# Layer norm scaling moved from VectorE to GpSimd, behind its own power, in a four-layer gated attention kernel

## The reference

```
def _layernorm(x, axis=-1, eps=1e-05):
    m = jnp.mean(x, axis=axis, keepdims=True)
    v = jnp.var(x, axis=axis, keepdims=True)
    return (x - m) / jnp.sqrt(v + eps)
...
    x = x + jnp.tanh(g_xattn[0]) * _L0_xattn_ref(_layernorm(x, axis=-1), ...)
    x = x + jnp.tanh(g_ffn[0]) * _L0_ffn_ref(_layernorm(x, axis=-1), ...)
```

## Time and profile before

| | |
|---|---|
| time, three runs | 2367.44 us median (2361.81 to 11244.14) |
| the profiled execution | 2362.89 us, span 2360.8 us, mean TensorE clock 0.952 |
| busy | PE 2068.2, PEld 1614.0, DVE 1973.1, ACT 1476.0, POOL 959.0 us |
| HEADS block, one pass | 136.5 us |
| WIDE block, one pass | 136.5 us |

### The profile page before, as it was taken

The page is one execution under the profiler, slowest core; times in us unless marked ns, Lnnn a source line. Parts: engine busy times, 40 slices in busy tenths (PEclk is TensorE's granted clock), DMA queues, the critical chain, the costliest instruction groups (busy, mean ns, idle before and its releaser), DMA issues. The chain is left out here.

```text
span 2360.8 us, 41642 instructions
## 1 busy us (share of the span) xinstructions
PE 2068.2 (88%) x12569; PEld 1614.0 (68%) x12569; DVE 1973.1 (84%) x7820; ACT 1476.0 (63%) x3639; POOL 959.0 (41%) x1382
## 2 busy tenths in 40 slices
PE   5878788989989899989999899998999899797767
PEld 3556567657966688656876578765886578666545
DVE  1299897989989798998989898897989899896971
ACT  3546467666767666776666666676667767476431
POOL 3233214543354424554164434544255432433432
PEclk9979899999999999999999999999999999899877
DMA  4000101010100101001100101001100001001000
GB/s 184 1 8 1 34 24 32 1 34 1 55 4 1 34 19 39 1 1 35 55 3 1 34 6 52 1 1 34 32 26 1 6 23 55 30 4 52 1 3 3
DMA packets 29503, 55.03 MB, mean 23 GB/s; under 512 B 2914, under 2 KB 10082, under 8 KB 28642
## 3 DMA queue, kind: packets, MB, share of 16 engines
q1 hardware_dynamic: 29282, 52.37, 6.8%
HBM read 51.31 MB, written 1.05 MB: 22 GB/s over the span
## 5 line engine op out<-in xcount | busy, mean ns | idle before, releaser
L232 DVE MATCH_REPLACE8 top_work<-top_eight,top_work 128x256 f32<-128x256 f32 x1664 | 668.4, 409 | 0.0
L234 DVE MAX8 top_eight<-top_work 128x8 f32<-128x256 f32 x1664 | 618.0, 413 | 0.2
L268 POOL TENSOR_TENSOR top_p<-top_p,top_rest 128x512 f32<-128x512 f32 x192 | 244.4, 1273 | 161.4 <-ACT top_rest L261 161.4
L789 PE MATMUL bank<-workP 128*128 128x256 f32 x1024 | 275.5, 393 | 12.4 <-ACT att_pP L927 10.2
L927 ACT ACTIVATE att_pP<-bank,att_tinyP 128x256 f32<-128x256 f32 x512 | 216.0, 480 | 57.1 <-DVE att_tinyP L976 55.3
L789 PEld LDWEIGHTS bank<-workP 128*128 128x128 f32 x1024 | 179.4, 192 | 62.2 <-issue 30.7
L976 DVE TENSOR_REDUCE att_tinyP<-bank 128x2 f32<-128x512 f32 x256 | 173.7, 682 | 25.5 <-PE bank L789 23.5
L234 DVE MAX8 top_lead<-bank 128x8 f32<-128x256 f32 x384 | 145.1, 420 | 42.1 <-PE bank L594 17.8
L261 ACT ACTIVATE top_rest<-top_work,top_nmax 128x256 f32<-128x256 f32 x384 | 173.3, 503 | 11.2 <-DVE top_work L232 10.9
L240 POOL TENSOR_SCALAR top_nmax<-top_lead 128x2 f32<-128x2 f32 x192 | 37.1, 193 | 346.4 <-DVE top_lead L234 345.9
L949 POOL TENSOR_SCALAR workP<-workP,const 128x256 f32<-128x256 f32 x256 | 121.7, 482 | 128.3 <-PE bank L789 106.2
(11 more groups left out here) (335 smaller groups left out, 4646.3 us busy)
## 6 DMA issues: line engine op xcount, KB each, us to landing
gelu_w<-in_pack3w SPq DMA_DIRECT2D x72, 256.0 KB, 3.0
top_qk<-in_pack3w SPq DMA_DIRECT2D x72, 256.0 KB, 2.8
pack<-in_pack SPq DMA_DIRECT2D x1, 4352.0 KB, 19.8
pack<-in_pack SPq DMA_DIRECT2D x1, 2266.0 KB, 9.9
pack<-in_pack SPq DMA_DIRECT2D x1, 1028.0 KB, 7.5
mix_wb<-in_ctx SPq DMA_DIRECT2D x1, 1024.0 KB, 4.9
x_in<-in_x SPq DMA_DIRECT2D x8, 128.0 KB, 2.2
ctx_tok<-in_ctx SPq DMA_DIRECT2D x8, 128.0 KB, 2.4
```

The costliest lines, as they stand in the source:

```text
L232: ins = nc.vector.match_replace(self.work[:, u % 2, j, :], eight, src, GONE)
L234: ins = nc.vector.max(eight, src)
L268: self.k.nc.gpsimd.tensor_tensor(v, v, self.rest[:, :, :], ALU.subtract).then_inc(self.p_ready, 1)
L789: mm = self.k.nc.tensor.matmul(self.banks[u % 2][:, j * T:(j + 1) * T], self.q1[:, u % self.RING, j * P:(j + 1) * P], self.kT, start=True, ...
```

## The change

`dve_scale` goes, and its two instructions are issued on GpSimd in `LayerNorm.pool`, behind the power and a wait for the power's own semaphore. The nine calls of `dve_scale` at step 1 are removed. No order string is touched. Semaphores, buffers and the other engines' instructions stay as they were.

```
-    def dve_scale(self, dve):
-        dve.wait_ge(self.rstd_ready, 1)
-        for j in range(NT):
-            self.k.nc.vector.tensor_scalar(self.y[:, j, :], self.x[:, j, :], self.mv[:, j, 0:1], self.rstd[:, j:j + 1],
-                                           ALU.subtract, ALU.mult).then_inc(self.y_ready, 1)
-
     def pool(self, pool):
         pool.wait_ge(self.var_ready, 1)
-        self.k.nc.gpsimd.tensor_tensor(self.rstd[:, :], self.var[:, :], self.k.half[:, 0:NT],
-                                       ALU.pow).then_inc(self.rstd_ready, 1)
+        nc = self.k.nc
+        nc.gpsimd.tensor_tensor(self.rstd[:, :], self.var[:, :], self.k.half[:, 0:NT], ALU.pow).then_inc(self.rstd_ready, 1)
+        pool.wait_ge(self.rstd_ready, 1)
+        for j in range(NT):
+            nc.gpsimd.tensor_scalar(self.y[:, j, :], self.x[:, j, :], self.mv[:, j, 0:1], self.rstd[:, j:j + 1],
+                                    ALU.subtract, ALU.mult).then_inc(self.y_ready, 1)
...
-        if s == 1:
-            self.ln.dve_scale(dve)
```

## The result

The changed kernel takes 2412.45 us (median of 6 runs, 2408.23 to 2417.94) against 2366.11 for the kernel before in the same comparison: ratio 1.020, 95% interval 1.0182 to 1.0218. One of the six runs of the kernel before took 11244.14 us and is left out of the ratio; without it their median is 2364.79. The change makes the kernel slower by 46 to 48 us, where 2359 (2346 to 2373) was forecast. The profiled execution took 2413.05 us, its span is 2411.2, the mean granted clock 0.936 (0.952 before).

What follows compares the result with a forecast made beforehand. VectorE and TensorE, both nearly full, were taken to hand the critical path back and forth. From 2362.9 us, -6.3 in the loop, -1.3 outside and +4.0 for configuration gave 2359.3, so 2359 us, range 2346 to 2373.

Steps and rivals of the forecast that it cites:

- relief carries on: Rival, whole kernel: work VectorE finishes earlier also speeds the other engines; 2327 us at half of 71 us; chance 0.20.
- I take 0.41, ends 0.375 and 0.456: GpSimd's price in us for one 128-column scaling instruction, interpolated from other instructions in the trace.
- +0.26 each: Five norms outside the loop where TensorE waits: y's second half from 0.64 to 0.90 us, +1.3 us in all.
- priced at +0.15: First norm of WIDE, each of six passes: TensorE turns y's second half about 0.15 us later.
- the four priced as gains of 0.60: Four norms outside the loop in VectorE stretches: 0.60 us saved at each, -2.4 us in all.
- the two priced at -0.68: Two norms outside the loop, VectorE's pair held up by GpSimd: second half at 0.90 instead of 1.58 us, -1.4 in all.
- WIDE's third norm, -1.20: Inside a VectorE stretch in each of six passes: 1.58 us freed, gain limited to TensorE's 1.20 us wait.
- HEADS, "All 0": HEADS in the loop: VectorE's savings and the later GpSimd work at its four norms change the time by 0.
- hidden by 0.08 us: Performer in HEADS: L240 shifts by 0.90 us but had idled 0.98 us, so no cost.
- The configuration, +4.0: GpSimd's setup ahead of its first TENSOR_SCALAR, no longer covered: +4.0 us, bounds 0 and 5.4.
- GpSimd becomes late: Rival: 0.90 us delays on GpSimd hold up following work; 2372 us, or 2402 at 0.9 us an instruction; chance 0.22.
- if they take 0.7 or more, the losing side wins: Sign to check: GpSimd's 128 scaling instructions taking 0.7 us or more, not about 0.41, would mean a slower kernel.

Runs made afterwards that it cites:

- y not late: Changed kernel, but TensorE and the mixed attention's squares on ScalarE read x behind the power, GpSimd's pair going unread: 2373.38 us against 2367.79, ratio 1.0016.
- pair of 2 columns: Changed kernel with GpSimd's two instructions over 2 of the 128 columns only: 2360.72 us, ratio 0.9971 to the kernel before.
- add form: Changed kernel, but VectorE writes the negated mean and GpSimd adds and multiplies, at all norms: 2368.41 us against 2366.53 for the kernel before, ratio 1.0008.
- filler in the waits: Changed kernel with seven extra, overwritten transposes of x on TensorE at the 42 norms where it waits: 2388.99 us, ratio 1.0100 to the kernel before.
- subtract form: Kernel before with GpSimd subtracting the mean and multiplying at only the 14 one-bank gated-expert and GELU-expert norms: 2368.67 us against 2367.1, ratio 1.0002.
- pricing run: Kernel before with twelve more unused GpSimd instructions in its setup: from the first block on, TensorE busy 10.6 us longer and idle 1.6 us less.

## Why the prediction was wrong, step by step

- **What bounds the kernel.** Right that VectorE's time is worth little: with y not late and VectorE relieved of the pair, the kernel was no faster than before (1.0016). The "relief carries on" rival, 2327, had 0.20 and is out; in the changed kernel VectorE's idle time in HEADS grew from 14.7 to 19.7 us.
- **What an instruction costs on GpSimd.** This step failed. "I take 0.41, ends 0.375 and 0.456" against 0.79. The interpolation and both its ends ran through instructions that multiply or add, so the range did not hold the subtraction. The run with the pair of 2 columns and the one with the add form show that the 46 us hang on this step. The Trainium skill (GPSIMD Engine Reference, Engine selection) gives about twice VectorE's time with two inputs and roughly line rate with one. The estimate from the first, 686 ns, was the nearer one by luck, since this instruction has one input tensor; the second fits the multiply (0.30 to 0.45 us against VectorE's 0.34) and not the subtract (0.79).
- **The clock.** The sum has no term for it. TensorE's busy time for the same matmuls grew by 34 us between the profiled executions, and filler in the waits gave 23 us back: about half of the loss.
- **y's halves.** They were forecast at 0.49 and 0.90 us behind the power and came at 0.91 and 1.69. Every term at a norm for which TensorE waits follows: "+0.26 each" at the five became +1.05; at WIDE's first norm, priced at +0.15, the second turn went from 0.70 to 1.73. At places priced at 0 the second turn became later too: in WIDE's M lane (1.06 to 1.74) and its last norm (1.03 to 1.75). So it did at the four priced as gains of 0.60 (331 and 2117 from 0.69 to 1.74, 171 and 2032 from some 1.2 to some 1.74), and the two priced at -0.68 gained nothing (1.63 to 1.74).
- **WIDE's third norm, -1.20.** The wait went, as forecast: in the changed kernel the transposes behind VectorE's L2093 start with no idle time, where the earlier trace rows has 1.20:

```profile
1186.87 0.61 DVE L2093 TENSOR_SCALAR mix_rest<-mix_rest,mix_rden 128x256 f32<-128x256 f32 x2
```

```profile
1188.29 0.60 PE L118 MATMUL bank<-const,mix_rest 128*128 128x128 f32 x4
```

  What that is worth is less clear. With the subtract form moved in WIDE at this norm alone, the block lost 0.4 us of idle time and not 1.2, and 1.4 more by a higher clock.
- **HEADS, "All 0".** Idle time +1.0, and 1.6 of clock, which the forecast didn't count. It looked there for what VectorE saves and for what follows on GpSimd, and left out y itself: in the trace before TensorE waits for it 0.04 us at the third norm and 0.88 at the fourth, and with the change their second halves are turned 1.73 to 1.75 us behind the power instead of 0.69.
- **The Performers.** In HEADS L240 was "hidden by 0.08 us" at 0.90; at 1.66 the cover is gone, and L240 of the earlier trace rows starts straight behind the copy:

```profile
1233.68 1.57 POOL L318 TENSOR_SCALAR yP<-x_in,ln_mvP,ln_rstdP 128x128 f32<-128x128 f32 x2
1235.22 0.61 POOL L458 TENSOR_TENSOR att_pTP<-ctxT 128x256 f32<-128x256 f32 x1
1235.77 0.40 POOL L459 COPY att_vP<-ctx_tok 128x256 f32<-128x256 f32 x1
1236.14 0.19 POOL L240 TENSOR_SCALAR top_nmax<-top_lead 128x2 f32<-128x2 f32 x1
```

  The 8 alone cost 6 to 7 us, timed. That run's busy time is 14.1 us above before's profiled execution and its idle time equal; against the pricing run the 5.2 us are 3.5 busy and 1.7 idle. So how much of it is waiting is not settled.
- **The configuration, +4.0.** It cost nothing that shows. The same place as the earlier trace rows, after:

```profile
19.14 0.70 POOL L315 TENSOR_TENSOR ln_rstdP<-ln_varP,minus_half 128x2 f32<-128x2 f32 x1 [2.30 <-DVE ln_varP L310]
19.95 1.58 POOL L318 TENSOR_SCALAR yP<-x_in,ln_mvP,ln_rstdP 128x128 f32<-128x128 f32 x2
21.50 0.61 POOL L458 TENSOR_TENSOR att_pTP<-ctxT 128x256 f32<-128x256 f32 x1
...
22.16 1.22 PE L372 MATMUL bank<-att_pTP,const 128*128 128x256 f32 x2 [2.03 <-POOL att_pTP L458]
```

  The first TENSOR_SCALAR starts 0.11 behind the power's end, with the MODIFY_POOL_CONFIG between; at the later norms, which have none, it is 0.10 to 0.12. Taking the upper end because "the only row that has it leaves that much room" was no evidence: the room in the earlier trace rows was the wait for ScalarE. The 6 us of the Trainium skill (GPSIMD Engine Reference, Instruction dispatch) for the first call of freshly loaded code don't show at this instruction. TensorE's L372 is 1.62 later instead of the +0.90 of the sum, again the price.
- **The rival "GpSimd becomes late".** Its case with 0.9 us an instruction gave 2402 and was the nearest, in mechanism as in time. It took the second half's lateness at some 30 norms, with no clock. The count was 44, and about half of the loss came with the clock. That 2402 is as near as it is owes something to luck: it has 5.4 us for the configuration and a price above 0.79, and lacks 14 norms and the clock.

Of the signs named in the prediction, "if they take 0.7 or more, the losing side wins" worked. WIDE, which was to shrink by about 1 us, grew by 1.3, and HEADS, which was to stay within 0.3, grew by 2.6.

## What to carry to other kernels

The price of a TENSOR_SCALAR on GpSimd belongs to its operation as well as to its shape: interpolate only between rows with the same operation, or measure it, and let the range hold a factor of two where no such row exists.

Before moving a step, list when its reader comes: 14 norms, 12 of them with a reader 2.5 us or more behind the power, were worth 10 us with a cheap form; the 42 with a waiting reader cost 35 us with the dear one.

In this kernel TensorE's longer waits cost twice, once as idle time and once as slower matmuls. So compare busy time at an equal count of matmuls before a loss is put down to waits. But compare it between more than one execution of each kernel: two executions of the same blocks differed by 10.6 us of busy time here, as much as several of the effects looked for.

## What the runs showed of the hardware

- On GpSimd a TENSOR_SCALAR of 128x128 fp32 with subtract and multiply takes 0.64 (numbers), 0.71 (one tile operand) or 0.79 us (two), with multiply and multiply 0.30, 0.37 or 0.45, and with add and multiply 0.44 in the program. The mean could be negated on VectorE for one instruction of 128x2.
- The first MODIFY_POOL_CONFIG adds no time that the trace shows (0.11 us from the power's end to the next start, with it and without).
- The same 12569 matmuls held TensorE busy for 2068 us before and 2102 after, with 226.5 and 311.9 us at the lower clock. In two executions of the same blocks, 12560 matmuls took 2066 and 2076 us.
- On ScalarE an ACTIVATE Identity of 128x128 fp32 with scale and bias from tiles takes 0.49 us.
- Recorded durations on VectorE can grow with no slowdown. The best-of instructions before and after, busy us and mean ns:

```profile
L232 DVE MATCH_REPLACE8 top_work<-top_eight,top_work 128x256 f32<-128x256 f32 x1664 | 668.4, 409 | 0.0
L234 DVE MAX8 top_eight<-top_work 128x8 f32<-128x256 f32 x1664 | 618.0, 413 | 0.2
```

```profile
L232 DVE MATCH_REPLACE8 top_work<-top_eight,top_work 128x256 f32<-128x256 f32 x1664 | 681.4, 426 | 0.0
L234 DVE MAX8 top_eight<-top_work 128x8 f32<-128x256 f32 x1664 | 630.8, 429 | 0.2
```

  Each is some 16 ns longer, yet from the end of one MAX8 to the end of the next, where they follow within 0.6 us, it is 326 ns at the median both before and after. Why the records grew is open; no time is to be charged for it.
